# Reordering ScalarE's copy of transposed probabilities and VectorE's low halves in a split-precision attention and expert kernel

## The reference

```
x = x + tanh(g_xattn) * attention(layernorm(x), ctx, ctx)
x = x + tanh(g_ffn)   * top2_of_3_experts(layernorm(x))

attention: q = n @ Wq (32 heads of 128), k = ctx @ Wk, v = ctx @ Wv (8 key/value heads)
           q, k = rotated by position (rope)
           scores = q k^T / sqrt(128), masked; p = softmax(scores); o = p v; o @ Wo
experts:   act_e(h @ w1[e] + b1[e]) @ w2[e] + b2[e], act = tanh, gelu, silu; two experts
           per batch, chosen from a softmax over h and the ratio of mean magnitudes
```

## Time and profile before

| | us |
|---|---|
| median of 3 runs | 773.21 (770.47 to 775.34) |
| the profiled execution, its own time | 772.14 |
| its span, first to last instruction | 770.1 |
| TensorE busy | 733.0 (95%) |
| VectorE busy | 552.4 (72%) |
| GpSimd busy | 417.6 (54%) |
| ScalarE busy | 362.9 (47%) |
| mean granted TensorE clock | 0.989 of full |

### The profile page before, as it was taken

One profiled execution on the slowest core, in us unless ns is written; L12 is line 12 of the kernel. 1 busy time (PEld: TensorE's weight loads), 2 busy tenths in 40 slices (PEclk: granted clock), 3 DMA queues, 4 the chain that ended last, 5 costly groups with the idle time before them and its releaser, 6 DMA issues.

```text
span 770.1 us, 11366 instructions
## 1 busy us (share of the span) xinstructions
PE 733.0 (95%) x3574; PEld 607.6 (79%) x3574; DVE 552.4 (72%) x907; ACT 362.9 (47%) x956; POOL 417.6 (54%) x352
## 2 busy tenths in 40 slices
PE   5899899899999999999999999999998799799998
PEld 4677688788888888888888888888876677688886
DVE  4967887688787878788787878788789845532224
ACT  4422443554545554555545554555546666024220
POOL 5654425575666666575666666665664345045220
PEclk9999999999999999999999999999999999899999
DMA  7794465322221222032131122122222211020002
GB/s 274 227 316 177 163 237 168 111 77 66 72 79 60 59 79 82 30 107 64 45 106 60 54 82 82 54 83 64 75 73 65 82 39 45 14 55 1 1 14 96
DMA packets 65534, 70.04 MB, mean 91 GB/s; under 512 B 8528, under 2 KB 42320, under 8 KB 65488
## 3 DMA queue, kind: packets, MB, share of 16 engines
q1 hardware_dynamic: 65104, 68.46, 28.3%
q0 software_dynamic: 384, 1.05, 0.4%
HBM read 50.61 MB, written 18.87 MB: 90 GB/s over the span
## 4 chain that ended last, share of the span: by engine, by line
PE 80%; DVE 10%; issue 4%; POOL 4%; ACT 1%; DMA 0%; SPq 0%; POOLq 0%; ACTq 0%; DVEq 0%
PE y L229 32%; PE q L239 31%; PE o L569 5%; PE s L517 5%; PE pt L439 4%; PE s L519 2%; DVE scores L1208 1%; POOL roped L939 1%; DVE nmr L1189 1%; DVE rot L1046 1%; DVE rot L1047 1%; DVE rot L1045 1%; POOL prob L979 1%; POOL scores L939 1%; ACT prob L812 1%
## 5 line engine op out<-in xcount | busy, mean ns | idle before, releaser
L229 PE MATMUL y<-wb_hi,split 128*128 128x512 f32 x512 | 176.3, 405 | 1.6 <-DVE split L1018 1.6
L239 PE MATMUL q<-xT_hi,wa_hi 128*128 128x512 f32 x352 | 141.6, 402 | 0.0
L239 PE MATMUL q<-xT_lo,wa_hi 128*128 128x512 f32 x352 | 137.9, 392 | 0.0
L239 PE MATMUL q<-xT_hi,wa_lo 128*128 128x512 f32 x352 | 137.8, 392 | 0.0
L966 POOL TENSOR_TENSOR roped<-rot 128x512 f32<-128x512 f32 x59 | 76.6, 1298 | 106.8 <-DVE rot L1047 106.8
L229 PEld LDWEIGHTS y<-wb_hi,split 128*128 128x128 f32 x512 | 96.9, 189 | 21.1 <-DVE split L1018 1.8
L800 ACT ACTIVATE cT_hi<-roped 128x512 fp32r<-128x512 f32 x64 | 40.5, 633 | 141.3 <-POOL roped L966 137.2
L812 ACT ACTIVATE prob<-scores,nmax 128x128 f32<-128x128 f32 x256 | 100.0, 392 | 14.9 <-DVE nmax L1152 14.9
L979 POOL TENSOR_TENSOR prob<-prob,prec 128x512 f32<-128x512 f32 x64 | 66.7, 1042 | 70.5 <-DVE prec L1166 70.5
L229 PE MATMUL y<-wb_lo,split 128*128 128x512 f32 x256 | 100.5, 393 | 0.0
L970 POOL TENSOR_TENSOR cT_lo<-roped,cT_hi 128x512 fp32r<-128x512 f32 x64 | 83.3, 1301 | 12.9 <-ACT cT_hi L800 12.9
(11 more groups left out here) (152 smaller groups left out, 1524.2 us busy)
## 6 DMA issues: line engine op xcount, KB each, us to landing
k_scratch<-split SPq DMA_DIRECT2D x16, 512.0 KB, 3.7
v_scratch<-split SPq DMA_DIRECT2D x16, 512.0 KB, 3.7
wraw<-in_L_xattn_Wq SPq DMA_DIRECT2D x32, 256.0 KB
wraw<-in_L_xattn_Wo SPq DMA_DIRECT2D x32, 256.0 KB
kv<-k_scratch SPq DMA_DIRECT2D x64, 128.0 KB, 2.5
kv<-v_scratch SPq DMA_DIRECT2D x64, 128.0 KB, 2.7
wraw<-in_L_ffn_w SPq DMA_DIRECT2D x24, 256.0 KB
rows<-ctx_t SPq DMA_DIRECT2D x8, 256.0 KB, 5.5
```

What stands on the lines that cost most here:

```text
L229: mm = pe.matmul(bank_[:, :], stationary(s, c), moving(m, c), start=(c == 0 and n == 0), stop=(c == EC - 1 and n == 2))
L239: mm = pe.matmul(bank_[:, :].rearrange("p (b t) -> p b t", b=BH), weights[s][:, c, h * P:(h + 1) * P], source[m][:, half * BH:(half + 1) * ...
```

## The change

The lists of ScalarE and VectorE change; those of TensorE, GpSimd and SyncE do not. In the units, ScalarE's copy of the transposed probabilities moves from behind the query tile's copy to right behind the copy of `o`, ahead of the weight chunk. In the opening, VectorE subtracts a value tile's low half ahead of the rotation of the next tile and no longer behind it. And the context pieces 4 to 7 are split at m = 1, 2, 4, 6, and no longer at m = 1, 2, 3, 4, on both engines; on VectorE a piece now comes behind a key tile's low half. TensorE transposes the probabilities behind the scores and the query projection in both kernels.

```diff
--- before.py
+++ after.py
@@ -65,6 +65,7 @@
 FILL = LAG_S
 LN_AT = (9, 11, 13, 16)
 X_AT = 20
+PIECE_AT = (1, 2, 4, 6)
 PIECES = 2 * EC
 W_PER = 2 * EC
 W_B = 4 * EC
@@ -730,8 +731,8 @@
                 w_hi_to(n)
             for m in range(TILES_A):
                 keys, _, _, n = tile_a(m)
-                if 1 <= m <= EC:
-                    c_hi_(EC + m - 1)
+                if m in PIECE_AT:
+                    c_hi_(EC + PIECE_AT.index(m))
                 if m >= X_AT:
                     row_hi_(m - X_AT)
                     if m - X_AT + 2 < B:
@@ -772,6 +773,11 @@
                     if not (isinstance(g, int) and i - LAG_Y < 1):
                         act.wait_ge(y_done, i - LAG_Y)
                     act.activation(split[:, 2, 0, :], obank[:, :], ACT.Copy).then_inc(o_hi, 1)
+                if has(LAG_P):
+                    act.wait_ge(p_t, i - LAG_P + 1)
+                    if past >= LAG_P + 1:
+                        act.wait_ge(o_done, i - LAG_P)
+                    act.activation(split[:, 1, 0, :], pbank[:, :], ACT.Copy).then_inc(p_hi, 1)
                 if not drain:
                     if b == 0 and past >= B:
 
@@ -798,11 +804,6 @@
                     if past >= B:
                         act.wait_ge(s_done, s_done_before(i - 1, bq))
                     act.activation(q_split(0, bq // BH, bq % HG), roped[:, :], ACT.Copy).then_inc(q_hi, 1)
-                if has(LAG_P):
-                    act.wait_ge(p_t, i - LAG_P + 1)
-                    if past >= LAG_P + 1:
-                        act.wait_ge(o_done, i - LAG_P)
-                    act.activation(split[:, 1, 0, :], pbank[:, :], ACT.Copy).then_inc(p_hi, 1)
                 if has(LAG_S):
                     act.wait_ge(s_max, i - LAG_S + 1)
                     if past >= LAG_S + 1:
@@ -1071,6 +1072,8 @@
                 w_lo_(n)
             for m in range(TILES_A):
                 keys, half, k, n = tile_a(m)
+                if m >= 1 and not tile_a(m - 1)[0]:
+                    tile_lo(m - 1)
                 if keys:
                     if n == 0:
                         dve.wait_ge(rope_ok, 2)
@@ -1081,10 +1084,10 @@
                         dve.wait_ge(rope_ok, 4)
                     dve.wait_ge(k_proj, n + 1)
                     rotate(qbank[n % 2], k // HG, k_rot)
-                if 1 <= m <= EC:
-                    c_lo_(EC + m - 1)
-                if m >= 1:
+                if m >= 1 and tile_a(m - 1)[0]:
                     tile_lo(m - 1)
+                if m in PIECE_AT:
+                    c_lo_(EC + PIECE_AT.index(m))
                 if m in LN_AT:
                     for t in (2 * LN_AT.index(m), 2 * LN_AT.index(m) + 1):
                         dve.wait_ge(x_in[t], 16)
```

## The result

The changed kernel takes 789.0 us in the median of 4 runs (788.69 to 790.95), the kernel before 773.24 on the same chip (770.47 to 775.34). The ratio is 1.021, with a 95% interval of 1.018 to 1.025: 15.8 us slower, where 15.9 had been summed. The profiled execution took 788.72, its span is 786.9 and so 16.8 longer than that of before; that the medians lie only 15.8 apart is the scatter of the executions.

The account below looks back on a forecast made before the run. TensorE, busy 95% of the span, was taken to bound the kernel. Units 8.1, opening 7.7, fill -0.4 and drain 0.5 make 15.9 us on the profiled 772.1: 788.0, so a median of 789 us, range 778 to 796.

Parts of the forecast that it names:

- ScalarE's copy can't be earlier than its input: Units: the copy of `pt` still waits for TensorE's transposes, gains nothing, delays the weight chunk; exponentials 0.8 us later.
- rival 3: Units: VectorE's 0.4 us margin before the output projection is used up, a hole in every unit: 11 us more, 800; chance 0.08.
- The units: Scores wait for GpSimd's low half of the query tile in one unit of four: 14 holes of 0.58, 8.1 us.
- K4 and piece 7: Opening: K4's last matmuls wait for the last context piece, split at 46.8; K4's rotation comes 6.1 us later.
- The value halves in VectorE's chain: Opening: low halves of V3 to V6 now lengthen VectorE's chain, +2.4 us; K6's copy slot wait gives back 0.8.
- V8's hole: Opening: TensorE's hole of 3.36 us at 80.37 goes, but TensorE then waits in front of the row transposes.
- Fill: First output product: the copy of `pt` at the head can follow VectorE's maximum, so -0.4 us.
- Drain: First drain unit: the output projection waits for the low half of `o`, 0.55 late: +0.5 us.
- rival 1: The opening loses, the units don't, as GpSimd's low half comes in time: 780.9 us; chance 0.12.
- rival 2: The units lose, the opening doesn't, as gains at V2 and V8 offset K4's wait: 781.4 us; chance 0.06.
- rival 4: Opening: V2 and V8 holes vanish, nothing replaces them, if the last piece is split by about 36.7: 765.6 us; chance 0.05.
- rival 5: Nothing measurable: TensorE transposes behind the scores as described, or losses as hidden as gains: 773 us; chance 0.05.

Follow-up runs that it names:

- Kernel 1: The kernel before with only ScalarE's copy of the transposed probabilities moved to right behind the copy of `o`: 783.6 us, ratio 1.0155.
- Kernel 3: The kernel before with that ScalarE copy moved and TensorE's transposes right behind the scores, ahead of the query projection: 767.95 us, ratio 0.9932.
- kernel 4: The kernel before with ScalarE's copy of the transposed probabilities between the weight chunk's and the query tile's copies: 769.56 us, ratio 0.9973.
- kernel 11: The changed kernel with TensorE's transposes moved right behind the scores: 775.5 us, ratio 1.004.
- Kernel 5: The kernel before with only the value tile's low half ahead of the next rotation, context pieces and units as before: 776.41 us, ratio 1.0065.
- kernel 2: The kernel before with only the opening's part of the change (value halves and context pieces), units as before: 780.91 us, ratio 1.0111.
- kernel 6: The kernel before with only the context pieces at m = 1, 2, 4, 6 behind the tile's low half: 775.52 us, ratio 1.0033.
- kernel 8: The kernel before with GpSimd's expert weight chunk in the drain ahead of the scaling, after VectorE's `nmr` step: 765.02 us, ratio 0.9899.

## Why the prediction was right, step by step

**ScalarE's copy can't be earlier than its input: right, shown.** It waits 3.50 us where it had not waited, and the engines behind it are late by what was worked out: exponentials 2.17 after the start of the transposes where it had been 1.41 (forecast 0.8 later). No output projection waits in the units, so rival 3 is out.

**The units: mechanism right, size too small.** 8.1 was forecast, 11.4 came (7.40 to 18.78 late in 56 units). The count of 14 was right, and so was the path: 3.77 from the end of the transposes to the end of GpSimd's low half in the forecast (306.93 to 310.70) and in the trace (318.49 to 322.26). Mis-sized was the term for a hole, "TensorE stands until 310.70 + 0.06". The handover was 0.24 (322.26 to 322.50), and a hole costs 0.74 from start to start, not 0.54 (the 0.58 that the profile lists begins at the modelled end of the product before). The stalled unit itself ran another 0.10 slow in its first products, not 0.05. 12 x 0.84 and 2 x 0.65 make 11.4. Kernel 1 has the same loss without the opening's edit, and in kernels 3, 4 and 11, where the weight chunk is no longer late, it is gone. Why 0.24 is not shown: TensorE's transposes in the drain start 0.05 after GpSimd's scaling ends (596.38 to 596.43).

**K4 and piece 7: right, by two errors that met.** Piece 7 was split by 45.44 and not at 46.8: K2's rotation began at 31.14 where I had 31.7, and each of the two pairs of low half and piece took some 0.3 less than the 3.0 that I took (K3's 2.68, from 42.76 to 45.44). So K4's rotation came 4.9 late and not 6.1. But I counted three slow matmuls behind the hole of 6.41, and twelve ran at half clock, 0.43 from start to start until 50.35. Nine of them are K5's, whose rotation had to wait 2.27 for them and came 5.78 late (45.87 to 51.65): 0.9 us that the sum lacks. The windows' granted clock from 45.50 to 50.30 is 0.50 of full, the lower of the two levels (1.2 of 2.4 GHz).

**The value halves in VectorE's chain: right, shown.** 2.4 - 0.8 = 1.6 was forecast. From K5's rotation to the row transposes 1.56 was measured (5.78 to 7.34 late). K5 to K6 takes 0.56 more, K7 to K8 and K9 to K10 some 0.6 each; K6 to K7 takes 0.16 less, as a value half is put in and the slot's wait goes (0.8). Kernel 5 has these without the pieces. The sum at the row transposes is 4.9 + 0.88 + 1.56 = 7.34 for a forecast of 7.7. That V8's hole would go was not quite so: 1.23 of it is left, with no effect on the sum, since TensorE waits another 2.96 behind it for the same chain.

**Fill: the mechanism was right, the gain did not come.** VectorE's low half of `pt` now follows its maximum at once and is 0.45 earlier within its chain. The hole is still 2.87, because the whole chain began 0.48 later behind the first scores. VectorE's addition for the last tile, before and after:

```profile
130.70 1.14 DVE L1134 TENSOR_TENSOR roped<-rot 128x512 f32<-128x512 f32 x1
```

```profile
139.77 1.68 DVE L1137 TENSOR_TENSOR roped<-rot 128x512 f32<-128x512 f32 x1 [0.20 <-POOL cT_lo L971]
```

GpSimd's weight chunk starts at 130.00 and 139.63, so 1.14 us of the addition lie beside it now and 0.59 before. Kernels 1 and 2 show the two parts: hole 2.42 with the copy alone, 3.40 with the opening alone.

**Drain: right in the sum.** A loss of 0.5 in the first unit was forecast. Its output projection starts 0.51 later in the unit (596.57 behind a wait of 1.35), as forecast. It then ran partly at half clock (granted 0.71 of full from 595.00 to 599.00), so the unit took 8.69 and not 6.60; the next two gave that back (5.57 and 6.42 where it had been 6.75 and 6.86), and at the fourth unit's scores 0.47 is left (18.78 to 19.25). Kernel 1 does the same (8.68), kernel 2 does not (6.62).

**What was left out: the clock gives and takes.** Behind the wait of 2.96 us eight of the twelve products ran slow (the twelve take 91.39 to 95.83, 4.44 us, and took 2.85 before): +1.6. Behind the first output product's hole of 2.87 it was the other way. Before, TensorE ran slow after it (granted 0.76 of full from 141.90 to 144.90); in the change it had 1.00 from 150.80 to 153.80, and 1.5 us came back. At the router the same happened once more:

```profile
679.92 0.50 PE L230 MATMUL y<-wb_hi,cT_hi 128*128 128x512 f32 x1 [2.55 <-DVE xacc L1285]
680.26 0.39 PE L230 MATMUL y<-wb_lo,cT_hi 128*128 128x512 f32 x1
```

Before, the wait for `xacc` had been 4.42 and the products behind it stood 0.43 apart; now the slow products lie ahead of the wait, where the wait absorbs them, and behind it TensorE is at full clock. That is 19.05 to 16.82, 2.2 us back. So the sum was nearly exact because its units were 3.3 too small, the clock, left out, gave 2.2 back at the router, and the medians lie 1.0 closer than the two traces. I had the right steps with a lucky sum; by position, 19.25 late in the drain, it was 3.4 short.

**The rivals.** 1 and 2 each describe half of it, and kernels 2 and 1 show that both halves lose. 4 failed at the point that it named: piece 7 was split by 45.44, not by 36.7; and kernel 5 shows that V2's hole, taken away without that, is worth nothing. 5 is out: TensorE's list stayed, and kernels 3 and 11 show what its move would have done.

## What to carry to other kernels

A copy can't be moved ahead of its producer: move the producer first, or all one gets is a wait at the head of an engine's list, and the price is read from what is queued behind it, not from the wait (kernel 4 waits 3 us in each unit at no cost, the change 3.5 us at 11). In a stage that one chain of engines paces, as VectorE's did in this opening, an instruction put into that chain is lost and one moved into its waits is gained, and closing a hole on an engine that the chain paces only moves the hole. So first find where the pacing engine stands idle. And when a wait is taken away by swapping two instructions, ask who needs the one that is now second.

## What the runs showed of the hardware

- TensorE's clock behind a hole does not follow from the hole's length. After waits of 2.84 (V2) and 2.96 us it ran at half clock, after 3.36 (V8) and, in the change, 2.87 us it did not, while before the change it did after 2.87. In kernel 6 V8's wait of 3.35 was followed by half clock, and the same wait before was not. Each such case is worth 1.4 to 2.2 us, so two traces can be apart by that where the edits differ in nothing else.
- At the router there are two outcomes. In all fourteen traces the router's wait was either 4.42 to 4.43 with slow products behind it, or 2.35 to 2.55 with full clock behind it and slow products ahead.
- An instruction of VectorE for one element per partition took 1.24 us beside a GpSimd subtraction that had begun 0.06 earlier, and 0.16 without it (kernel 8). Its end, 598.16, is that of the subtraction, 598.15. In the opening a VectorE subtraction of 512 elements with both operands in on-chip SBUF took 0.94 to 1.75 us beside one of GpSimd, for 0.69 alone. At 33.22, where VectorE's came first, it took 0.69, and GpSimd's addition from 33.27 took 1.77 for 1.29. In the units the low half of `o`, which is read from the bank `o`, took 0.69 at 304.97 with GpSimd's addition running from 305.02.
- The first product of 512 columns behind scores or transposes takes 0.28 to 0.32 us to the next where 0.23 is usual. Kernel 3 has one such place less in each unit, and its units take 7.49 for 7.55.
